# Building the two head-halves of a scan chunk one after the other, before either is multiplied

## The reference

```python
xn = _layernorm(x)
zxbcdt = xn @ in_proj_w.T                 # 2048 z, 2048 x + 64 B + 64 C, 16 dt
# a branch; run forward, and on the reversed sequence with its own weights
xBC = _causal_conv_silu(xBC, conv_w, conv_b)          # 4 taps
def step(h, inp):                          # 16 heads of 128, state 64
    x_t, dt_t, B_t, C_t = inp
    dA = jnp.exp(dt_t * A)
    h = h * dA[:, :, None, None] + jnp.einsum('bh,bhp,bn->bhpn', dt_t, x_t, B_t)
    y = jnp.einsum('bhpn,bn->bhp', h, C_t)
    return (h, y)
y = scan(step) + D * x
yz = y * silu(z);  y = yz * rsqrt(mean(yz * yz) + EPS) * norm_w
s = (y_fw + y_bw) @ out_proj_w.T
g = silu(quantised_matmul(xn, weight) + bias)
out = x + s * g
```

## Time and profile before

| | |
|---|---|
| median of 3 runs | 7708.97 us (7705.66 to 7710.78) |
| the profiled execution | 7721.43 us |
| its span, core 4, the slowest | 7719.9 us (cores from 7683.0 to 7719.9) |
| TensorE busy | 2630.6 us, 34% |
| VectorE busy | 2879.1 us, 37% |
| ScalarE busy | 1293.4 us, 17% |
| mean granted TensorE clock, core 4 | 0.583 of full speed |

### The profile page before, as it was taken

How to read it: one execution, slowest core, us unless ns; L and a number is a source line. 1 busy time by engine, 2 the same in 40 slices (tenths; PEclk the granted TensorE clock), 3 DMA queues, 4 the chain that set the end, 5 groups by cost and what they waited for, 6 DMA issues and landing times.

```text
span 7719.9 us, 45099 instructions; the slowest of 8 cores (7683.0 to 7719.9 us)
## 1 busy us (share of the span) xinstructions
PE 2630.6 (34%) x11640; PEld 1256.3 (16%) x11752; DVE 2879.1 (37%) x5634; ACT 1293.4 (17%) x1843; POOL 125.5 (2%) x234
## 2 busy tenths in 40 slices
PE   0133334343333334114234333422522432342353
PEld 0011111121111111002112111211211211121121
DVE  2533333334333333053343344244334334424432
ACT  0011111121121111011111111111121111111111
POOL 0000000000000000000000000000000000000000
PEclk9855555555555555556566556556556655555555
DMA  4110000011011100620010011001001001100100
GB/s 87 41 32 26 26 26 26 27 31 32 26 32 29 31 26 18 129 57 24 17 40 28 20 31 33 29 17 38 24 17 40 28 20 31 33 29 17 38 24 17
DMA packets 364329, 250.33 MB, mean 32 GB/s; under 512 B 319456, under 2 KB 321761, under 8 KB 355890
## 3 DMA queue, kind: packets, MB, share of 16 engines
q0 software_dynamic: 30448, 132.95, 5.7%
q1 hardware_dynamic: 297216, 74.76, 5.0%
q10 hardware_dynamic: 36418, 39.72, 1.6%
HBM read 117.33 MB, written 68.19 MB: 24 GB/s over the span
## 4 chain that ended last, share of the span: by engine, by line
DVE 35%; PE 26%; DMA 14%; ACT 12%; issue 11%; DVEq 1%; ACTq 1%; POOLq 0%; POOL 0%; SPq 0%
PE ps L239 26%; DVE qv L424 6%; DVE convX L432 3%; DMA u<-u 2%; DMA sflat<-s_scr 2%; ACT mtq L695 2%; ACT convX L771 2%; DVE convX L404 2%; ACT gq L678 2%; ACT convX L509 2%; ACT Xtm L1272 2%; DMA b3c<-s_scr 1%; DVEq L75 1%; DVE convX L410 1%; DVE bwq L699 1%
## 5 line engine op out<-in xcount | busy, mean ns | idle before, releaser
L239 PE MATMUL ps<-convBC 64*128 64x128 bf16 x64 | 16.8, 262 | 2551.0 <-DVE um L371 1334.7
L699 DVE TENSOR_TENSOR bwq<-Btm,mtq 128x512 bf16<-128x512 bf16 x128 | 88.7, 693 | 1890.7 <-ACT mtq L695 1890.7
L239 PE MATMUL ps<-xnT,warena 128*128 128x256 bf16 (+2 forms) x4480 | 603.4, 298 | 391.2 <-DMA xnT<-xn 195.9
L239 PE MATMUL ps<-mtq,Xtm 128*128 128x128 bf16 x1024 | 287.3, 281 | 973.1 <-DVE mtq L734 868.2
L239 PEld LDWEIGHTS ps<-xnT,warena 128*128 128x128 bf16 (+2 forms) x4480 | 451.0, 107 | 546.7 <-issue 453.5
L424 DVE TENSOR_TENSOR qv<-stgX,cwX 128x1012 bf16<-128x1012 bf16 x384 | 465.6, 1212 | 40.0
L239 PEld LDWEIGHTS ps<-convBC 64*128 64x128 bf16 x64 | 6.4, 100 | 2568.2 <-issue 2568.2
L764 ACT CAST hT<-ps 64x512 bf16<-64x512 f32 x256 | 148.2, 579 | 1559.3 <-PE ps L239 1559.3
L239 PE MATMUL ps<-sflat,ones 3*64 3x512 bf16 (+1 forms) x512 | 282.5, 602 | 363.7 <-ACT gq L678 177.0
L239 PE MATMUL ps<-warena,Xtm 128*128 128x512 bf16 x992 | 292.2, 463 | 236.6 <-DVE Xtm L1321 138.6
L239 PE MATMUL ps<-Xtm,bwq 128*64 128x128 bf16 x1024 | 320.5, 313 | 0.0
(11 more groups left out here) (149 smaller groups left out, 3931.7 us busy)
## 6 DMA issues: line engine op xcount, KB each, us to landing
u<-u POOLq DMA_DIRECT2D x64, 512.0 KB, 4.3
sp_x<-stgX POOLq DMA_DIRECT2D x16, 1024.0 KB, 4.2
sp_y<-convX POOLq DMA_DIRECT2D x16, 1024.0 KB, 4.6
stgX<-sp_x POOLq DMA_DIRECT2D x16, 1024.0 KB, 5.6
ybw<-sp_y POOLq DMA_DIRECT2D x16, 1024.0 KB, 5.1
ur<-u POOLq DMA_DIRECT2D x32, 512.0 KB, 4.0
out<-ostg ACTq DMA_DIRECT2D x64, 256.0 KB, 2.0
warena<-ipw POOLq DMA_DIRECT2D x1, 4352.0 KB, 32.7
```

The lines of the kernel that those rows point to most:

```text
L239: lambda e: e.matmul(out_ap, lhsT, rhs, start=start, stop=stop),
L699: lambda e: e.tensor_tensor(v["bwq"][:].rearrange("p (h n) -> p h n", h=8), v["Btm"][:, c, :].unsqueeze(1).broadcast_to([128, 8, 64]), v[" ...
```

## The change

The loop over the two halves is split in two. The first loop builds the operands of half 0 and then those of half 1; the second does the bursts and copies of half 0 and then of half 1. Half 1 needs its own `mtq`, `gq`, `bwq` and `diagq`: they lie in the memory of `ur` and `ostg`, two f32 tiles of pass B's output stage, read as bf16. `gcq` has one buffer, so that the product for half 1 (L718 before) moves behind the bursts of half 0, with a wait for them. G now goes to the same PSUM region as D and the output. The `bwq` product has one wait more, for the queue of the output DMA (`qo`), which reads `ostg`.

```diff
+            urb = v["ur"][:].bitcast(BF16)
+            ostb = v["ostg"][:].bitcast(BF16)
+            mtq2 = urb[:, 0:1024]
+            gq2 = urb[0:64, 1024:2048]
+            bwq2 = ostb[:, 0:512]
+            diagq2 = ostb[0:64, 512:1024]
...
+            ph = []
             for hq in range(2):
                 h0 = hq * 8
                 pd = 1024 + 1024 * (q_rot[0] % 2)
                 q_rot[0] += 1
-                py = 1024 + 1024 * (q_rot[0] % 2)
...
-                mm(ps[0:64, gsl], v["ones3"][cb0:cb0 + 3, 0:64],
+                mtq_h = v["mtq"][:] if hq == 0 else mtq2
+                gq_h = v["gq"][:] if hq == 0 else gq2
+                bwq_h = v["bwq"][:] if hq == 0 else bwq2
+                diagq_h = v["diagq"][:] if hq == 0 else diagq2
+                mm(ps[0:64, pd:pd + 512], v["ones3"][cb0:cb0 + 3, 0:64],
                    v["sflat"][cb0:cb0 + 3, h0:h0 + 4, :], True, True,
                    wait=["qd", "ts", ("tv", tvm)])
...
                 p.op("scalar",
-                     lambda e: e.activation(v["mtq"][:], ps[:, dsl], AF.Exp),
+                     lambda e, mtq_h=mtq_h, dsl=dsl: e.activation(
+                         mtq_h, ps[:, dsl], AF.Exp),
                      wait=[("tp", t2v), "tv"], inc="ts")
...
-                     wait=[("ts", mtv), ("ts", cbv), "tv"], inc="tv")
+                     wait=[("ts", mtv), ("ts", cbv), "tv", "qo"],
+                     inc="tv")
...
+                if hq == 0:
+                    p.op("vector",
+                         lambda e: e.tensor_tensor(
+                             v["gcq"][:].rearrange("p (h t) -> p h t", h=8),
+                             v["gq"][:].rearrange("p (h t) -> p h t", h=8),
...
                 opv = p.mark("tv")
+                ph.append((h0, pd, mtq_h, gq_h, bwq_h, diagq_h, opv))
+            for hq in range(2):
+                h0, pd, mtq_h, gq_h, bwq_h, diagq_h, opv = ph[hq]
+                if hq == 1:
+                    ymv0 = p.mark("tp")
+                    p.op("vector",
+                         lambda e, gq_h=gq_h: e.tensor_tensor(
+                             v["gcq"][:].rearrange("p (h t) -> p h t", h=8),
+                             gq_h.rearrange("p (h t) -> p h t", h=8),
+                             v["convBC"][0:64, 1, csl].unsqueeze(1)
+                             .broadcast_to([64, 8, 128]),
+                             op=ALU.mult),
+                         wait=[("tp", ymv0), "tv"], inc="tv")
+                    opv = p.mark("tv")
                 for half4 in range(2):
                     sev = p.mark("ts")
```

More of the change, by code:

```diff
@@ L665, in scan_chunk @@
                 q_rot[0] += 1
-                py = 1024 + 1024 * (q_rot[0] % 2)
                 dsl = slice(pd, pd + 1024)
                 cb0 = 32 * c
-                gsl = slice(py, py + 512)
-                g2sl = slice(py + 512, py + 1024)
-                mm(ps[0:64, gsl], v["ones3"][cb0:cb0 + 3, 0:64],
+                mtq_h = v["mtq"][:] if hq == 0 else mtq2
[3 more added lines that the diff above has]
+                mm(ps[0:64, pd:pd + 512], v["ones3"][cb0:cb0 + 3, 0:64],
                    v["sflat"][cb0:cb0 + 3, h0:h0 + 4, :], True, True,
                    wait=["qd", "ts", ("tv", tvm)])
-                mm(ps[0:64, g2sl], v["ones3"][cb0:cb0 + 3, 0:64],
+                mm(ps[0:64, pd + 512:pd + 1024],
+                   v["ones3"][cb0:cb0 + 3, 0:64],
                    v["sflat"][cb0:cb0 + 3, h0 + 4:h0 + 8, :], True, True)
@@ L677, in scan_chunk @@
                 p.op("scalar",
-                     lambda e: e.activation(v["gq"][:],
-                                            ps[0:64, py:py + 1024], AF.Exp),
+                     lambda e, gq_h=gq_h, pd=pd: e.activation(
+                         gq_h, ps[0:64, pd:pd + 1024], AF.Exp),
                      wait=[("tp", t1v), "ts", ("tv", tvm)], inc="ts")
@@ L698, in scan_chunk @@
                 p.op("vector",
-                     lambda e: e.tensor_tensor(
-                         v["bwq"][:].rearrange("p (h n) -> p h n", h=8),
+                     lambda e, bwq_h=bwq_h, mtq_h=mtq_h: e.tensor_tensor(
+                         bwq_h.rearrange("p (h n) -> p h n", h=8),
                          v["Btm"][:, c, :].unsqueeze(1).broadcast_to(
                              [128, 8, 64]),
-                         v["mtq"][:].rearrange("p (h t) -> p h t", h=8)[
+                         mtq_h.rearrange("p (h t) -> p h t", h=8)[
                              :, :, anchor:anchor + 1].broadcast_to(
@@ L706, in scan_chunk @@
                          op=ALU.mult),
-                     wait=[("ts", mtv), ("ts", cbv), "tv"], inc="tv")
+                     wait=[("ts", mtv), ("ts", cbv), "tv", "qo"],
+                     inc="tv")
                 p.op("vector",
-                     lambda e: e.tensor_tensor(
-                         v["diagq"][:].rearrange("p (h n) -> p h n", h=8),
+                     lambda e, diagq_h=diagq_h, gq_h=gq_h: e.tensor_tensor(
+                         diagq_h.rearrange("p (h n) -> p h n", h=8),
                          v["i64"][:].unsqueeze(1).broadcast_to([64, 8, 64]),
-                         v["gq"][:].rearrange("p (h t) -> p h t", h=8)[
+                         gq_h.rearrange("p (h t) -> p h t", h=8)[
                              :, :, anchor:anchor + 1].broadcast_to(
@@ L716, in scan_chunk @@
                      wait=["tv"], inc="tv")
-                p.op("vector",
[L718 to L728, removed]
+                if hq == 0:
[6 more added lines that the diff above has]
+                             op=ALU.mult),
+                         wait=["tv"], inc="tv")
+                p.op("vector",
+                     lambda e, mtq_h=mtq_h: e.tensor_tensor(
+                         mtq_h.rearrange("p (h t) -> p h t", h=8),
+                         mtq_h.rearrange("p (h t) -> p h t", h=8),
                          v["cbt"][:].unsqueeze(1).broadcast_to(
@@ L733, in scan_chunk @@
                 p.op("vector",
-                     lambda e: e.tensor_tensor(
-                         v["mtq"][:], v["mtq"][:],
+                     lambda e, mtq_h=mtq_h, h0=h0: e.tensor_tensor(
+                         mtq_h, mtq_h,
                          v["ddiag"][:, h0 * 128:(h0 + 8) * 128], op=ALU.add),
@@ L751, in scan_chunk @@
                         mm(ps[:, ysl], xop,
-                           v["mtq"][:, hh * 128:(hh + 1) * 128], True, False,
+                           mtq_h[:, hh * 128:(hh + 1) * 128], True, False,
                            wait=w0)
@@ L756, in scan_chunk @@
                         ssl = slice(3584 + hh4 * 128, 3584 + (hh4 + 1) * 128)
-                        mm(ps[0:64, ssl], v["bwq"][:, hh * 64:(hh + 1) * 64],
+                        mm(ps[0:64, ssl], bwq_h[:, hh * 64:(hh + 1) * 64],
                            xop, True, False)
                         mm(ps[0:64, ssl],
-                           v["diagq"][:, hh * 64:(hh + 1) * 64],
+                           diagq_h[:, hh * 64:(hh + 1) * 64],
                            hTa[:, h * 128:(h + 1) * 128], False, True)
```

## The result

Over 8 runs of each, the changed kernel takes 7175.69 us (7166.34 to 7184.74) and the kernel before 7710.55. The ratio is 0.9305, with a 95% interval from 0.9295 to 0.9315: 535 us less. The forecast was 7185 us.

A forecast was written before the change was run, and what follows sets the result against it. The prediction saw a string of hand-overs with no engine short of throughput. 64 chunks at 8.20 us save 525 us, 7721.43 to 7196, times 0.9984 gives 7185 us; range 7145 to 7245, 8 in 10.

The forecast's parts named there:

- The net of a chunk: Scan chunk: 11.19 us gained less 2.99 lost, net 8.20, so a pass A chunk goes from 43.83 to 35.6 us.
- the stated bound: Three starts after a ScalarE operation: 0.24 us each taken, 0.14 to 0.63 possible, -19 to +75 us in all.
- Steps 1 and 2: Half 1's `mtq` starts 6.06 us after half 0's ends; VectorE's five for half 0 finish 1.96 us before needed, hidden.
- The price of the added wait: Output-queue wait on `bwq`: hidden in the slack; with cover gone, below 0.1 us a chunk.
- Step 3: Burst of half 0 waits for `mtq` of half 1, starting at 7.33 instead of 4.34: costs 2.99 us a chunk.
- Steps 4 and 5: Under half 0's burst, VectorE's four tiles take 3.1 of 8.36 us; moved `gcq` ends some 0.6 us early; both hidden.
- Step 6: Burst of half 1 starts 0.24 us after half 0's output copy, where 11.43 passed before: gains 11.19 us.
- Doesn't change: Work around the chunk, such as `cbt`, the wait for `pro` and the last copy, was claimed to stay as it was.
- The build behind VectorE: First rival: half 1's build starts only after VectorE finishes half 0; net 4.10 us a chunk, 7447 us; chance 0.05.
- Full clock in the scan: Rival: TensorE gets full clock in the scan, saving 650 us more, 6535 us; chance 0.04.
- Loss of clock in the projections: Rival: projections lose their full clock, taking 960 us more, 8145 us; chance 0.02.

The follow-up runs named there:

- the first rival's kernel: Changed kernel with G of half 1 also waiting for all VectorE work ahead of it, the five operations of half 0: 7427.86 us, ratio 0.9633.
- two banks: Changed kernel with two PSUM banks for the new state, so a half's second 16 matmuls skip the first state copy: 7053.21 us, ratio 0.9148.
- the version with all waits gone: Changed kernel with bursts waiting on half 0's `mtq` and state copy, two PSUM banks, half 1's `gcq` product in its build: 6848.59 us, ratio 0.8887.

## Why the prediction was right

**The net of a chunk.** Forecast 8.20 us, found 8.40. G of half 1 starts 0.24 after `mtq` of half 0 and its own `mtq` at 6.06 (1735.35 - 1729.29), both as written. The two bursts start 0.14 after their releaser and not 0.24: that is the 0.20 us. It was in the stated bound (0.14 to 0.63). The 0.24 was taken from rows where ScalarE's count is not the last of the list; in the burst's list it is, and waits listed ahead of it are over by then. The release is shown by the rows; that the place in the list makes the difference is an argument, which two experiments bear out: the burst released by VectorE, whose count comes first, starts 0.24 after `gcq`, and in the first rival's kernel, where VectorE's count stands at the end of G's list and is the one that comes last, G starts 0.14 after VectorE (1758.57 0.14 issue, 1758.70 G). No run changed the place in the list alone.

**Steps 1 and 2, the hidden five.** Right, and sized: two operations more cost nothing, five more came onto the path by 2.21 us a chunk. 3.95 us of added work less 2.21 makes a slack of 1.74, hand-over counted; the prediction had 1.96 without it. The price of the added wait with its cover gone, "below 0.1 us a chunk", is right for the one half that it speaks of, 0.07; with the order taken back the wait is on the path in both halves and costs 0.14.

**Step 3, the cost.** The burst of half 0 was forecast 2.99 us later than before, counted from `mtq` of half 0. It is 1736.52 - 1729.29 = 7.23 against 4.34, 2.89. Taking off the wait for `mtq` of half 1 gave back 1.45 of it, 91 us in all. The sum puts the whole 2.99 on this wait; it did not say that G and D, ahead of the burst in TensorE's queue, would keep the other half even without it.

**Steps 4 and 5, hidden work under the burst.** VectorE's four took 3.07 us, and the burst kept its 3.75 us for 16 matmuls (3.74 before), so that VectorE under a burst costs TensorE nothing that shows. The slack of `gcq` was forecast at 0.6 and measured at 0.54.

**Step 6, the gain.** 11.43 us between output copy and burst before; 0.14 now. The order taken back brings 11.50.

**The stretches between the scans.** "Doesn't change" held for the mean but not for each core. The mean span of the eight cores went from 7698.0 to 7160.6 us, 537 less, where 64 x 8.40 = 538. The same core tells less: core 4 took 580 us less, core 0 500. That 7721.43 - 538 = 7183 is also what the profiled execution took, 7184.05, is partly luck, since the slowest is another core. The cores of that one execution lie between 7137.3 and 7182.5. The waits of cores 0 and 4 in it differ in the transfers (us in all, times, longest), core 0 first:

```profile
DVE bns L353 <- DMA u<-u: 341.9, 64, 7.0
DVE haloX L1222 <- DMA dtraw<-sp_dt: 189.4, 15, 14.1
ACT negA L329 <- DMA cwBC<-cw: 152.7, 1, 152.7
```

```profile
DVE bns L353 <- DMA u<-u: 328.0, 64, 7.0
DVE haloX L1222 <- DMA dtraw<-sp_dt: 177.7, 15, 12.9
ACT negA L329 <- DMA cwBC<-cw: 141.5, 1, 141.5
```

These three waits together are 37 us longer on core 0, and its span is 42 us longer. The first of them also goes with most of the 26 us that five `bwq` products more cost too little: VectorE's wait for `u` is shorter there on every core, 307.4 to 322.4 us against 327.2 to 345.6 in the changed kernel, and the means, 312.7 and 336.7, differ by 24. With two banks the mean is 326.8, so 10 of the 20 us that it gained too much. Why a core or a kernel waits more or less for its transfers wasn't tried.

**The rivals.** The build behind VectorE, forecast at 7447 us, took 7428 when made by hand. Full clock in the scan didn't come, in the changed kernel or with a stretch of 17.89 us. One chunk of the changed kernel, columns as in the earlier trace rows:

```profile
1721.00:1757.00 36.00, 23.76 (x81) 8.95 (x81) 7.18 (x12) 8.48 (x11) 0.00 (x0) 0.50 0.00 1
```

All 32 scans of this core show 0.50, and so do all 32 of core 7 in the version with all waits gone. Loss of clock in the projections didn't come either: the mean granted clock went from 0.583 to 0.594. About half of that rise is only the shorter span, for the same 1282 us at full clock, (0.583 - 0.50) / 0.50 of 7719.9, would make 0.589 of 7182.5; the rest is within what runs of the kernel before show on core 4 (0.583 to 0.588). The advice of the Trainium skill, "TensorE: Matmul & The Clock Gate", section "Why this matters for your kernels", to leave no long idle gaps between bursts was followed ever further in the experiments, and the scan's clock did not answer to it.

## What to carry to other kernels

Where an engine order is written out by hand and no engine is over half busy, count the pieces of one iteration on the chain of waits, and ask which of them need the piece before them and which only stand behind it in a queue or a count. Here two loops instead of one gave 7%, and waits for the operation needed in place of everything issued so far, with a second PSUM bank and one product made earlier, gave nearly 6% more. Give each rearrangement its price beside its gain: work brought forward sits in the queue ahead of what was first before, and here that took back 2.9 of 11.3 us a chunk.

## What the runs showed of the hardware that was not expected

- The granted clock stays at 0.50 through 17.89 us in which TensorE has no gap, while in the same kernel's projection the window behind the first 3 us shows 0.99. What makes the difference was not tried.
- In the rows of this case a hand-over from ScalarE to TensorE takes 0.14 us where ScalarE's count is the only or the last wait of the list, and 0.24 us where one more stands behind it (0.63 before the matmul of `cbt`, where three do); one wait more ahead of a VectorE operation whose inputs are just ready takes 0.07 us (0.30 instead of 0.23). That the place in the list is the reason is argued, not shown. The 0.10 us between the two hand-overs, at two starts, is the whole 0.2 us a chunk by which the forecast was off.
